# Matmuls whose results nobody reads, in the routing pass of a vision tower

## The reference

```python
h = _layernorm(h)                                   # 197 tokens x 192
xn = _rms_norm(h, norm_weight, RMS_EPS)
tok = _l2_normalize(xn)
sl = _l2_normalize(slots) * scale[:, None]          # 64 slots
logits = jnp.einsum('sd,btd->bst', sl, tok)
dispatch_w = jax.nn.softmax(logits, axis=-1)        # over tokens
combine_w = jax.nn.softmax(logits, axis=-2)         # over slots
y = jnp.einsum('btd,bst->bsd', xn, dispatch_w)
```

## Time and profile before

| what | us |
|---|---|
| median of three runs | 5439.64 |
| profiled execution, its own time | 5434.61 |
| its span from the first to the last instruction | 5432.6 |
| PE busy in the span | 5126.5 (94%) |
| DVE busy | 3312.5 (61%) |
| ACT busy | 2802.2 (52%) |
| POOL busy | 1822.5 (34%) |

### The profile page before, as it was taken

One profiled execution on the slowest core, in us unless ns is written; L12 is line 12 of the kernel. 1 busy time (PEld: TensorE's weight loads), 2 busy tenths in 40 slices (PEclk: granted clock), 3 DMA queues, 4 the chain that ended last, 5 costly groups with the idle time before them and its releaser, 6 DMA issues. The chain is left out here.

```text
span 5432.6 us, 157461 instructions
## 1 busy us (share of the span) xinstructions
PE 5126.5 (94%) x48514; PEld 4442.1 (82%) x48514; DVE 3312.5 (61%) x9370; ACT 2802.2 (52%) x7044; POOL 1822.5 (34%) x2821
## 2 busy tenths in 40 slices
PE   8999999799999999999979999999997888889988
PEld 7999999677777777777758888888886777779975
DVE  4555555566666666666646666666665666650047
ACT  3444444255555555555535555555554666663445
POOL 2333333233333333333322222222222444441135
PEclk9999999899999999999979999999998555559965
DMA  5777777666667667767746666666663222229977
GB/s 142 174 173 175 173 173 175 145 146 152 151 151 152 152 150 152 152 149 153 153 91 131 131 130 131 132 132 130 131 130 90 63 65 66 67 59 261 277 216 233
DMA packets 701720, 789.03 MB, mean 145 GB/s; under 512 B 362639, under 2 KB 514989, under 8 KB 701646
## 3 DMA queue, kind: packets, MB, share of 16 engines
q1 hardware_dynamic: 701646, 788.10, 62.8%
HBM read 518.50 MB, written 265.72 MB: 144 GB/s over the span
## 5 line engine op out<-in xcount | busy, mean ns | idle before, releaser
L710 DVE TENSOR_REDUCE a_mx<-a_sq 99x2 f32<-99x394 f32 x1536 | 798.2, 561 | 165.6 <-PE a_sq L764 160.1
L710 DVE TENSOR_REDUCE c_mx<-c_sq 99x2 f32<-99x198 f32 (+1 forms) x1536 | 656.3, 462 | 259.1 <-PE c_sq L764 245.0
L662 ACT ACTIVATE a_ex<-a_sk 99x792 f32<-99x792 f32 (+1 forms) x768 | 638.7, 832 | 204.4 <-PE a_sk L794 172.2
L662 ACT ACTIVATE c_ex<-c_sk 99x792 f32<-99x792 f32 (+1 forms) x768 | 511.0, 665 | 330.8 <-PE c_sk L794 225.8
L399 PE MATMUL e_tokp<-e_wmap,e_ptT 128*99 128x192 f32 x3072 | 531.0, 330 | 1.0 <-ACT e_ptT L304 1.0
L399 PEld LDWEIGHTS e_tokp<-e_wmap,e_ptT 128*99 128x99 f32 x3072 | 492.3, 167 | 2.5 <-ACT e_ptT L304 1.3
L764 PE MATMUL a_sq<-a_ks,a_qs 96*99 96x198 bf16 x3072 | 429.2, 254 | 40.6 <-DVE a_vx L694 28.2
L761 PE MATMUL c_sq<-c_maskb,c_identb 99*99 99x198 bf16 x1536 | 380.9, 260 | 39.8 <-DVE c_bout L700 26.3
L764 PE MATMUL c_sq<-c_ks,c_qs 96*99 96x99 bf16 (+1 forms) x3072 | 413.0, 230 | 0.0
L794 PE MATMUL a_sk<-a_qs,a_ks 99*99 99x198 bf16 (+1 forms) x3072 | 404.8, 253 | 6.8 <-issue 6.8
L863 PE MATMUL a_work<-a_hT,a_wqkv 96*96 96x198 f32 x2048 | 390.9, 333 | 4.5 <-DVE a_rest L725 2.5
(11 more groups left out here) (179 smaller groups left out, 11894.0 us busy)
## 6 DMA issues: line engine op xcount, KB each, us to landing
e_patches<-in_x SPq DMA_DIRECT2D x128, 588.0 KB
x_w<-in_fc SPq DMA_DIRECT2D x128, 576.0 KB, 5.8
scr_qk<-e_parts SPq DMA_DIRECT2D x128, 445.5 KB
scr_qk<-a_parts SPq DMA_DIRECT2D x128, 445.5 KB
scr_tv<-e_tv SPq DMA_DIRECT2D x128, 297.0 KB
a_tv<-scr_tv SPq DMA_DIRECT2D x128, 297.0 KB
scr_tv<-a_res SPq DMA_DIRECT2D x128, 297.0 KB
c_tv<-scr_tv SPq DMA_DIRECT2D x128, 297.0 KB
```

What stands on the lines that cost most here:

```text
L662: nc.scalar.activation(to, of, ACT.Exp).then_inc(exped.sem, 1)
L710: nc.vector.reduce_max(mx[:, b2.parity, qt, h:h + 2], sq[f % 2][:, :, 0:width], AX.X).then_inc(maxed.sem, 1)
```

## The change

TensorE gets matmuls whose results no instruction reads. A new tile `fill` (128 partitions x 640, bf16, set to 1.0 once by VectorE) gives both operands: 128 columns as weights, 512 columns streamed. The results go to a new PSUM tile `unread`. A helper issues them: one at the head of each TensorE step, one ahead of the dispatch product (L1175), one ahead of the product with the slots (L1194). In step 12 (DEPTH + 2) the one at the head is replaced by 24. They are issued in all 138 steps, whether the step's other parts are there or not. They wait for nothing and signal nothing. The semaphore `prep` gets one more increment, of the memset, and the numbers that are waited for on it move up by one. Nothing else is changed.

```diff
+        fill = m.sb("r_fill", [128, 640], BF16)
+        unread = m.ps("r_unread", [128, 512])
@@ gpsimd
-            pool.wait_ge(prep, 4)
+            pool.wait_ge(prep, 5)
@@ scalar
-            act.wait_ge(prep, 3)
+            act.wait_ge(prep, 4)
@@ vector
             nc.vector.memset(dw[:], 0.0).then_inc(prep, 1)
+            nc.vector.memset(fill[:], 1.0).then_inc(prep, 1)
...
-            dve.wait_ge(prep, 3)
+            dve.wait_ge(prep, 4)
@@ tensor
-            pe.wait_ge(prep, 5)
+            pe.wait_ge(prep, 6)
...
-            pe.wait_ge(prep, 6)
+            pe.wait_ge(prep, 7)
+
+            def keep_warm(times):
+
+                for _ in range(times):
+                    nc.tensor.matmul(unread[:], fill[:, 0:128], fill[:, 128:640], start=True, stop=True)
 
             def step(c):
                 b5, b6, b7, b9, b10 = c - 5, c - 6, c - 7, c - 9, c - 10
+                keep_warm(24 if isinstance(c.turn, int) and c.number == DEPTH + 2 else 1)
                 if b7.inside(n):
...
                     mm.then_inc(x_turned.sem, 1)
+                keep_warm(1)
                 if b10.inside(n):
...
                     mm.then_inc(w_turned.sem, 1)
+                keep_warm(1)
                 if b6.inside(n):
```

## The result

The changed kernel's profiled execution took 5281.41 us (span 5279.4), the kernel before 5434.61. Twenty executions of each were timed on the same chip: 5435.74 to 5455.29 us before, median 5443.81; 5281.41 to 5535.96 us after, median 5481.61. The ratio of 0.9739 (0.9716 to 0.9763) is made from the executions nearest the fastest alone, and here that leaves out what the spread is about: the median of all twenty is 0.7% above that of the kernel before. Sorted, the twenty are 5281, 5293, 5303; 5335, 5392, 5437; four from 5448 to 5454; ten from 5510 to 5536. The mean granted clock of an execution falls with its time, from 0.961 at 5281 us over 0.916 at 5450 to 0.894 at 5536; the twenty of the kernel before lie within 20 us of each other. So the change gains 2.6 to 3.0% where the clock holds to the end, and in ten of the twenty executions it loses 1.2 to 1.7%.

What follows compares the result with a forecast made beforehand. TensorE at 1.2 GHz was taken to bound the routing pass, 5.36 us an image. 5434.6 - 187.3 + 7.5 + 3.5 + 0.5 = 5258.8, plus 5.0 for the median, gave 5264 us; forecast 5240 to 5300, wider range 5240 to 5400.

Steps and rivals of the forecast that it cites:

- TensorE's ring: Routing pass: TensorE's products and transposes plus its wait for VectorE's scaling, 5.36 us an image, forecast 3.72 at full clock.
- then others are as late: Routing pass at full clock: VectorE and ScalarE were to limit the step about as much as TensorE, 3.67 to 3.72 us.
- VectorE's ring through GpSimd: Routing pass: VectorE's 2.86 us of work plus 0.81 until GpSimd's power lets its next step start, 3.67 us.
- the 3.72 and 3.67 of the sum: Routing step at full clock: 3.72 us for TensorE's ring, 3.67 for VectorE's ring through GpSimd.
- rival (d): Routing pass: clock stays up but other engines hold the step at 4.3 us or more; 5325 us, up to 5400; chance 0.13.
- ScalarE's 3.67 us a step: Routing pass: ScalarE's busy time per image, taken as one of three engines meeting at 3.67 to 3.72 us.
- ACT near full: Sign that the forecast is right: ScalarE almost fully busy in the routing pass, with steps of 3.7 to 3.9 us.
- The 24 and the filling: Added costs: +7.5 us for the burst in step 12, +3.5 for filling the pipeline, +0.5 for the memset.
- At least 3.2 of 3.8 us busy and no hole over 0.4: Routing step at full clock: TensorE's work and longest idle time, in us, from which the clock was expected to stay.
- Rival (a): Routing pass: clock never rises or falls again early; step 6.26 us, total 5564 us, 2.3% slower; chance 0.10.
- (b): Routing pass: clock falls at some middle image and stays down; between 5264 and 5564 us; chance 0.08.
- Rival (c): Routing pass: transposes, some 1.0 of 3.80 us a step, don't count as work for the clock; 5564 us; chance 0.04.

Runs made afterwards that it cites:

- e1_split: Changed kernel with the landings of a step's two stores told by two semaphores instead of one: 0.9669, 5243 to 5543 us.
- e7_half_rows: Changed kernel with three unread matmuls at each step's head instead of one, all unread matmuls reading 64 of 128 partitions: 1.0477, 5699 to 5726 us.
- e8_transposes: Changed kernel with 48 fp32 transposes of 128 x 128 at step 12 replacing the 24 matmuls, no other unread work: 5449.85 us.

## Why the prediction was right, and where it was wrong

- *The time*: 5264 us forecast, 5281 the fastest of twenty. Five of the twenty lie in the range of 5240 to 5400, the three that kept the clock and two that by their times kept it for over half of the steps; the median of all is 0.7% above the kernel before. That the ratio came out as forecast is owed to those few, and partly luck.
- *What bounds the pass*: right. TensorE's ring at 1.2 GHz was the bound, and at 2.4 GHz it is gone from VectorE's waits.
- *The price of a matmul*: 0.22 us at 2.4 GHz (4503.41 to the next group's start at 4503.63), 0.40 to 0.43 at 1.2, against 0.23 and 0.45. At the head they were free, up to three of them.
- *What the clock gives back*: L1205's eight (L1194 before) take 0.83 us instead of 1.59; the factor 0.56 was right within 0.04.
- *The step at the high clock*: 3.80 forecast, 4.07 measured. The step of the reasoning that failed is "then others are as late": I looked for VectorE's ring through GpSimd and did not follow the second wait of L1089, `stored`, to the DMA issued a step earlier; the description of the kernel before leaves that wait out too. With that wait split the step is 3.71 to 3.73, so the 3.72 and 3.67 of the sum were right. 122 x 0.27 = 33 us were lost to it; the 0.13 of rival (d) stood for such a thing, but as a vague sum of waits. ScalarE's 3.67 us a step, the third of the engines that were to meet, was too much: it is busy 246.67 of 300 us, 3.35 a step, in the changed kernel, and 3.32 in e1_split (267.77 of 300), so "ACT near full" did not come true.
- *The 24 and the filling*: step 12 starts 9.6 us late against 11.5 forecast. The steps after 134, taken as unchanged, and the passes behind them are 4.7 us shorter.
- *Does the clock rise*: yes, for the reason given. e7_half_rows shows the rows of the matmuls as what matters, as argued from the combining pass.
- *Does it stay*: wrong. "At least 3.2 of 3.8 us busy and no hole over 0.4" was taken as enough, from two falls that had followed holes. The holes became 0.7 us on average and 1.0 at most (52.0 us in 73 waits), since the step got longer and the matmuls faster, and PE was busy 3.2 to 3.4 of 4. With that the clock held to the end in 3 of 20 executions. Rivals (a) and (b) had 0.18 together and describe 17 of 20. A row at 2.60 of 4 us that kept the clock was one instance; the pass has to hold it in every one of 122 steps.
- *Rival (a)'s price*: 5564 forecast, 5521 to 5544 measured. The step at the low clock is 6.07 and not 6.26: the two matmuls add 0.71 us, not 0.90. Their own length explains 0.04 of the 0.19; the rest was not looked into.
- *Rival (c)*: transposes do lift the clock (e8_transposes), so its condition is false.

## What to carry to other kernels

Work that is added to hold a clock pays where it stands in a hole of the engine's own ring, and needs a margin: three unread matmuls a step kept it in 3 of 20 executions, five in all five. Time many executions, since one profile shows only one way it can go. When the bound gets faster, follow every semaphore of every wait in the loop, a shared count of two DMAs above all, because a ring of 4.04 us is invisible under one of 5.35. Splitting that semaphore was worth 0.7% after the change and nothing before it.

## What the runs showed of the hardware

A matmul burst of 64 rows, full for 10.42 us, left the clock at 0.50; 128 rows lifted it within the burst, and so did fp32 transposes of 128 x 128. The clock was lost with PE busy 3.19 of 4 us and a longest hole of 1.0 us, in a stream of steps of 3.8 to 4.4 us like those before it, and by the times not at the same place in each execution: 5448 to 5454 us is a group of four and 5510 to 5536 us one of ten. Why the clock goes at these places no run here explains.
